# Cross-attention scores in four row groups of 32 instead of two of 64, with the opening and the seam of a one-core transformer kernel reordered

## The reference, cut to what matters

```python
x = x + _L0_xattn_ref(_layernorm(x, axis=-1), ctx_1024, itok_BxS_0_255, ...)   # 4 layers, 16 heads of 8
x = x + _L0_attn_ref(_layernorm(x, axis=-1), ternary_factor_u, ternary_factor_v)
...
allowed = (j[None, None, :] <= seg_ids[:, :, None]) & (j[None, None, :] > seg_ids[:, :, None] - LOOKBACK)
cross_bias = jnp.where(allowed, 0.0, NEG)[:, None]
for l in range(N_LAYERS):
    h = rmsnorm(x, n1[l]); ...                       # self-attention with rotation, x = x + o
    qc = split_heads(rmsnorm(x, n2[l]) @ Wq_c[l].T, H)
    kc, vc = jnp.split(memory @ Wkv_c[l].T, 2, axis=-1)   # split in heads too
    x = x + merge_heads(sdpa(qc, kc, vc, cross_bias)) @ Wo_c[l].T
    h3 = rmsnorm(x, n3[l]); x = x + jax.nn.silu(h3 @ Wg[l].T) * (h3 @ Wu[l].T) @ Wd[l].T
```

## Time and profile before

| | before |
|---|---|
| device time, median of 3 runs (lowest to highest) | 500.36 us (498.7 to 501.63) |
| profiled execution: device time, span | 499.64 us, 497.5 us |
| PE matmul busy, share of the span | 465.2 us, 94% |
| PE weight load | 401.7 us, 81% |
| DVE | 358.0 us, 72% |
| ACT | 268.5 us, 54% |
| POOL | 227.9 us, 46% |

### The profile page before, as it was taken

The page is one execution under the profiler, slowest core; times in us unless marked ns, Lnnn a source line. Parts: engine busy times, 40 slices in busy tenths (PEclk is TensorE's granted clock), DMA queues, the critical chain, the costliest instruction groups (busy, mean ns, idle before and its releaser), DMA issues. The chain is left out here.

```text
span 497.5 us, 14297 instructions
## 1 busy us (share of the span) xinstructions
PE 465.2 (94%) x5430; PEld 401.7 (81%) x5430; DVE 358.0 (72%) x1025; ACT 268.5 (54%) x718; POOL 227.9 (46%) x342
## 2 busy tenths in 40 slices
PE   3899999999999999968999998899999998999997
PEld 3667887788778876967999887789999887689997
DVE  4395668566856786656887889999989987654643
ACT  4377757775777577614334475556466554442221
POOL 2871377137613851243799322767889322300000
PEclk9999999999999999979999999999999999999999
DMA  8601020101029000040210432031020000000000
GB/s 252 276 3 32 10 84 2 40 22 65 3 64 381 2 3 1 2 130 17 70 49 24 157 111 67 2 133 60 10 69 3 2 1 1 1 2 1 12 1 12
DMA packets 9953, 27.08 MB, mean 54 GB/s; under 512 B 1346, under 2 KB 4759, under 8 KB 9623
## 3 DMA queue, kind: packets, MB, share of 16 engines
q1 hardware_dynamic: 9878, 26.09, 15.5%
HBM read 25.82 MB, written 0.26 MB: 52 GB/s over the span
## 5 line engine op out<-in xcount | busy, mean ns | idle before, releaser
L913 POOL TENSOR_TENSOR rstd<-ss,par 128x1 f32<-128x1 f32 x52 | 28.5, 549 | 100.8 <-ACT sq L737 100.8
L759 ACT ACTIVATE pr<-sd 128x512 f32<-128x512 f32 x56 | 34.5, 626 | 5.4 <-DVE sd L816 4.9
L1243 POOL TENSOR_TENSOR xh<-xh,rsx 128x512 f32<-128x512 f32 (+1 forms) x32 | 29.8, 931 | 2.5
L1241 POOL TENSOR_TENSOR xh<-cx,mvx 128x512 f32<-128x512 f32 (+1 forms) x32 | 29.4, 918 | 2.7 <-DMA cx<-ctx_in 1.4
L741 ACT ACTIVATE h<-y,rstd 128x128 f32<-128x128 f32 x48 | 19.1, 399 | 9.5 <-POOL rstd L913 9.4
L1222 DVE BATCH_NORM_STATS2 stx<-cx 128x6 f32<-128x128 f32 x104 | 22.7, 276 | 0.5 <-DMA cx<-ctx_in 0.5
L1772 POOL TENSOR_TENSOR rstd<-mv,par 128x1 f32<-128x1 f32 x20 | 4.1, 207 | 39.8 <-DVE mv L1602 36.3
L737 ACT ACTIVATE sq<-y 128x129 f32<-128x129 f32 x52 | 15.9, 306 | 10.0 <-DVE y L847 8.6
L907 POOL TENSOR_TENSOR kblk<-qk,cf 128x512 f32<-128x512 f32 x20 | 20.8, 1040 | 0.9
L1232 POOL TENSOR_TENSOR rsx<-rsx,par 128x13 f32<-128x13 f32 x8 | 20.4, 2546 | 0.6
L1791 POOL TENSOR_SCALAR rk<-kss 128x8 f32<-128x8 f32 (+1 forms) x32 | 7.5, 235 | 24.0 <-DVE kss L1668 22.5
(11 more groups left out here) (570 smaller groups left out, 1507.2 us busy)
## 6 DMA issues: line engine op xcount, KB each, us to landing
cx<-ctx_in SPq DMA_DIRECT2D x13, 768.0 KB
we<-we_in SPq DMA_DIRECT2D x8, 514.0 KB, 7.1
wc<-wc_in SPq DMA_DIRECT2D x4, 768.5 KB, 5.8
wa<-wa_in SPq DMA_DIRECT2D x5, 387.0 KB, 3.0
wb<-wb_in SPq DMA_DIRECT2D x4, 256.5 KB, 3.8
uvT<-uvT_in SPq DMA_DIRECT2D x1, 1024.0 KB, 7.1
uv<-uv_in SPq DMA_DIRECT2D x1, 1024.0 KB, 8.6
cx<-ctx_in SPq DMA_DIRECT2D x13, 32.5 KB
```

What stands on the lines that cost most here:

```text
L759: nc.scalar.activation(pr[:, t, at:at + 512], sd[:, t, at:at + 512], ACT.Exp).then_inc(s[piece], 1)
L913: nc.gpsimd.tensor_tensor(rstd[:, t:t + 1], ss[:, t:t + 1], par[:, 1:2], ALU.pow).then_inc(s[piece], 1)
L1241: step(pool, "pool_step", nc.gpsimd.tensor_tensor(part, cx[u % 2][:, tiles, :], mvx[:, b, tiles, 0].unsqueeze(2).to_broadcast(shape), ALU. ...
L1243: nc.gpsimd.tensor_tensor(part, part, rsx[:, b, tiles].unsqueeze(2).to_broadcast(shape), ALU.mult).then_inc(xm["c_normed"], 1)
```

## The change

1. `cmask` and `cscores` go by four row groups of 32 rows (4 heads) in four banks, 128 columns each, in place of two of 64 rows and 256 columns. `kcblk` is half as wide, `cmax` and `cshift` read four banks, and PSUM is two tensors of four banks.
2. Opening: x is loaded first; the flag comes from a row of ids of its own (2 KB), the ids of all partitions are loaded late; `mem4` moves from ACT to DVE, behind the layer norm; the zeroing moves from ACT to POOL. The four `memory` pieces of layer 0 and what follows from them get places of their own (`FIRST`), inside layer 0.
3. Seam: on PE the general form now stands ahead of the fast branch (`falls="end"`). ACT leaves the fast branch after its last `tanh` and DVE after `z_norm` of tile 1; what is left of the seam (`rest`) is issued behind the branch.
4. New places in both tables. The `memory` pieces of layers 1 to 3 move behind the query projection, to just ahead of `cmask` or `gate`.
5. Semaphore names of the general form share those of the fast branch, and 17 increments go from DVE's opening to the general form.

```diff
-PERIOD, SKEW = 95.43, (0.0, 6.74, 13.36, 19.85)
+PERIOD, SKEW = 94.56, (0.0, 6.67, 13.36, 19.85)
...
+FIRST = {"memory": 13.27, "mem_k": 12.13, "mem_v": 15.39, "kc": 12.61}
...
-    2: {"project": ("shifta", "shiftb"), "cmask": ("cshift",), "gate": ("hidden",)},
+    2: {"project": ("shifta", "shiftb"), "gate": ("hidden",)},
+    4: {"cmask": ("cshift",)},
...
-    return l * PERIOD + PLACE[p] + SKEW[t]
+    return l * PERIOD + (PLACE[p] if l else FIRST.get(p, PLACE[p])) + SKEW[t]
...
-        self.first = {e: 1 + max(n for n, z in enumerate(q) if z[1] == 0) for e, q in self.queue.items()}
+        self.first = {e: 1 + max(n for n, z in enumerate(q) if z[1] == 0 and not (e == "ACT" and z[2] == LAYERS) and
+                                 not (e == "DVE" and z[2] == LAYERS and z[3:] != (1, "z_norm"))) for e, q in self.queue.items()}
+        self.rest = {z[2:] for e, q in self.queue.items() for z in q[self.first[e]:] if z[1] == 0}
...
-        sc = [ctx.enter_context(nc.psum_tensor(f"sc{i}", [P, 1024], F32)) for i in range(2)]
-        pt = ctx.enter_context(nc.psum_tensor("pt", [P, 1024], F32))
-        sm = ctx.enter_context(nc.psum_tensor("sm", [P, 1024], F32))
+        fours = [ctx.enter_context(nc.psum_tensor(f"four{i}", [P, 2048], F32)) for i in range(2)]
+        sc = [fours[0][:, 0:1024], fours[0][:, 1024:2048]]
+        pt, sm = fours[1][:, 0:1024], fours[1][:, 1024:2048]
...
         def sp_opening(sp):
-            sp.dma_start(segr[:], seg_in.to_broadcast([P, B * L])).then_inc(s["seg_loaded"], 16)
             sp.dma_start(x[:], x_in.rearrange("(t p) d -> p t d", p=P)).then_inc(s["x_loaded"], 16)
+            sp.dma_start(segi[:], seg_in).then_inc(s["row_loaded"], 16)
+            sp.dma_start(cf[:], cf_in).then_inc(s["cf_loaded"], 16)
+            load_a(sp, 0)
             sp.dma_start(memT[:], memT_in).then_inc(s["mem_loaded"], 16)
             load_b(sp, 0)
-            sp.dma_start(cf[:], cf_in).then_inc(s["cf_loaded"], 16)
-            load_a(sp, 0)
             sp.dma_start(trig[:], trig_in).then_inc(s["trig_loaded"], 16)
             sp.dma_start(cb[:], cb_in).then_inc(s["trig_loaded"], 16)
+            sp.dma_start(segr[:], seg_in.to_broadcast([P, B * L])).then_inc(s["seg_loaded"], 16)
...
         def pool_opening(pool):
+            for blocks in (vblk, vcblk):
+                nc.gpsimd.memset(blocks[:], 0.0).then_inc(s["zeroed"], 1)
...
-            act.wait_ge(s["mem_loaded"], 16)
-            nc.scalar.copy(mem4[:], memT[:].unsqueeze(2).to_broadcast([P, B, 4, KF])).then_inc(s["zeroed"], 1)
-            for blocks in (vblk[:].rearrange("p t b j a e -> p (t b j a e)"), vcblk[:].rearrange("p b g i e -> p (b g i e)")):
-                nc.scalar.activation(blocks, par[:, 2:3].to_broadcast([P, B * 4 * 4 * 9]), ACT.Copy, scale=0.0).then_inc(s["zeroed"], 1)
...
-            dve.wait_ge(s["seg_loaded"], 16)
-            nc.vector.tensor_copy(segf[:], segr[:]).then_inc(s["seg_steps"], 1)
+            dve.wait_ge(s["zeroed"], 2)
+            for a in range(2):
+                nc.vector.memset(vblk[64 * a:64 * a + 64, :, :, :, a, 8:9], 1.0).then_inc(s["zeroed"], 1)
+            for a in range(4):
+                nc.vector.memset(vcblk[32 * a:32 * a + 32, :, :, a, 8:9], 1.0).then_inc(s["zeroed"], 1)
+            dve.wait_ge(s["row_loaded"], 16)
+            nc.vector.tensor_copy(pts[0:1, 0, 0:B * L], segi[:]).then_inc(s["seg_steps"], 1)
             dve.wait_ge(s["x_loaded"], 16)
...
+            dve.wait_ge(s["mem_loaded"], 16)
+            nc.vector.tensor_copy(mem4[:], memT[:].unsqueeze(2).to_broadcast([P, B, 4, KF])).then_inc(s["mem_spread"], 1)
+            dve.wait_ge(s["seg_loaded"], 16)
+            nc.vector.tensor_copy(segf[:], segr[:]).then_inc(s["cmask_set"], 1)
...
-                for p in range(2):
-                    rows = slice(L * p, L * p + L)
-                    nc.tensor.matmul(bank[:, 512 * p:512 * p + 256], cmask[rows, P * t:P * t + P], it32[rows, :], start=True, stop=True)
+                for p in range(4):
+                    rows = slice(KF * p, KF * p + KF)
+                    nc.tensor.matmul(bank[:, 512 * p:512 * p + P], cmask[rows, P * t:P * t + P], it32[rows, :], start=True, stop=True)
...
-                    for p in range(2):
-                        rows = slice(64 * p, 64 * p + 64)
-                        last = nc.tensor.matmul(bank[L * b:L * b + L, 512 * p:512 * p + 256], qT[rows, t, L * b:L * b + L],
+                    for p in range(4):
+                        rows = slice(KF * p, KF * p + KF)
+                        last = nc.tensor.matmul(bank[L * b:L * b + L, 512 * p:512 * p + P], qT[rows, t, L * b:L * b + L],
                                                 kcblk[rows, 2 * t + b, :, :], start=False, stop=True, skip_group_check=True)
...
-        def either(eng, fast, whole):
+        def either(eng, fast, whole, falls="start"):
...
-            with eng.If(few == 1):
-                fast()
+            with eng.If(few == (1 if falls == "start" else 0)):
+                (fast if falls == "start" else whole)()
             with eng.Else():
-                whole()
+                (whole if falls == "start" else fast)()
...
-                either(pe, lambda: opening(pe, x_pe_piece, pe_piece, "PE"), whole)
+                either(pe, lambda: opening(pe, x_pe_piece, pe_piece, "PE"), whole, falls="end")
```

More of the change, by code:

```diff
@@ new lines @@
+    "PE": {"memory": -47.35, "turn1": -4.73, "project": 0.00, "values": 2.11, "causal": 11.71, "scores": 13.88,
+           "turna": 21.45, "turnb": 23.00, "weigha": 23.32, "weighb": 26.86, "turn_o": 29.26, "out": 31.67,
+           "turn2": 37.19, "qc": 39.18, "cmask": 41.54, "cscores": 41.61, "cturn": 51.03, "cweigh": 52.61,
+           "cturn_o": 56.05, "cout": 58.70, "turn3": 65.72, "gate": 67.21, "up": 71.13, "down": 80.29},
+    "ACT": {"square1": -10.18, "norm1": -6.78, "mem_k": -41.75, "hT1": -3.24, "q_groups": 11.96, "expa": 19.12,
+            "expb": 21.79, "turneda": 23.14, "turnedb": 24.18, "oT": 30.28, "square2": 32.70, "norm2": 35.24,
+            "hT2": 37.60, "qcT": 40.50, "cexp": 47.98, "cturned": 52.37, "coT": 55.16, "square3": 60.48,
+            "norm3": 61.34, "hT3": 66.18, "tanh": 69.35},
@@ L75 @@
+    "DVE": {"mem_v": -37.82, "rope": 2.26, "vblk": 7.71, "maxa": 17.73, "maxb": 17.93, "shifta": 18.38,
+            "shiftb": 19.12, "recip": 28.46, "o": 29.58, "y1": 31.93, "cmax": 43.40, "cshift": 48.07, "crecip": 55.27,
+            "co": 55.93, "y2": 59.63, "gated": 72.85, "hidden": 76.84, "y3": 79.93},
+    "POOL": {"pow1": -28.06, "rope_sum": -12.13, "rope_bias": -9.86, "k_groups": -8.09, "base": 5.09, "kc": 14.77,
+             "pow2": 11.92, "pow3": 43.90},
 }
 PLACE = {p: a for pieces in AT.values() for p, a in pieces.items()}
+FIRST = {"memory": 13.27, "mem_k": 12.13, "mem_v": 15.39, "kc": 12.61}
@@ L122 @@
 LAYER = {e: list(pieces) for e, pieces in AT.items()}
-FINAL = {"PE": {}, "ACT": {"square_f": 0.18}, "DVE": {"norm_f": 4.73, "x_f": 6.55, "z_moments": 10.88, "z_norm": 17.41},
-         "POOL": {"pow_f": -7.85, "z_power": 0.96}}
+FINAL = {"PE": {}, "ACT": {"square_f": 0.83}, "DVE": {"norm_f": 5.32, "x_f": 9.97, "z_moments": 11.56, "z_norm": 18.17},
+         "POOL": {"pow_f": 14.74, "z_power": 27.05}}
 for e in AT:
@@ L150 @@
+YEACH = 20.703
 YAT = {
[L151 to L160 removed]
@@ L942, in queue @@
             for _, l, t, p in od.queue[engine]:
-                if within(p, l):
+                if within(p, l) and (l, t, p) not in JOINT.rest:
                     piece_of(eng, od, p, l, t)
@@ L1812, in x_queue @@
             fresh = False
-            for _, _, i, g, p in JOINT.queue[engine][JOINT.first[engine]:]:
+            for _, kind, i, g, p in JOINT.queue[engine][JOINT.first[engine]:]:
+                if kind == 0:
+                    layer_of(eng, FAST, p, i, g)
+                    continue
                 if p not in EARLY and not fresh:
@@ L1879, in whole @@
                 def whole():
+                    for name in sorted(set(gsem) - {"ctx_loaded"}):
+                        dve.sem_inc(gsem[name], 1)
                     dve.wait_ge(s["iota_loaded"], 32)
```

128 lines of the change are left out of this document (63 added, 65 removed).

## The result

| | before | after |
|---|---|---|
| device time, median (lowest to highest) | 501.0 us (498.7 to 502.9) | 511.51 us (508.35 to 2416.88) |
| profiled execution: device time, span | 499.64, 497.5 us | 508.35, 506.3 us |
| PE matmul busy | 465.2 us, 94% | 460.8 us, 91% |

The account below looks back on a forecast made before the run. PE's issued work bounds the layers, chains of waits the opening and the seam. Opening 1.4, scores 2.9 and seam 2.0 sum to 6.3 us: 493.3 against the profiled 499.64, 494.0 against the median; range 490 to 499.5.

Parts of the forecast that it names:

- opening: Before the layers: 6.0 us from a shorter chain, less 0.9 branch delay and 3.7 for `memory`: 1.4 won, -0.7 to 2.6.
- layers: Layers: four row groups for the scores shorten PE's work, 2.9 us won, between 9.4 lost and 4.3 won.
- seam: Seam: PE without its branch starts `across` earlier and at a better clock; 2.0 us won, between 0 and 3.7.
- price of a far branch: Opening: PE reaching its fast branch behind the general form costs 2.9 us; `turn1` 0.9 late, delay bounded by 0 and 3.
- The scores: Layers: `cscores` from 0.59 to 0.37 and 0.05 off `cmask`, 0.27 us saved per tile, 4.3 us of PE.
- the 0.48 of slack: Layers: gap between `cshift` of tile 0 ending and the next `cmask` starting stays 0.48 us in either order.
- the two thirds: Layers: share of the split's 4.3 us of PE taken to reach the end, 2.9 us.
- My upper bound: Seam: at most 3.7 us, from `across` starting 2.5 earlier plus 1.2 that the low clock costs the first `across`.
- The rest: Later blocks: pieces swap with neighbours only; 0 us, within 1.
- the second: Rival: PE's branch costs 2.9 in the opening, ACT's and DVE's branches take the seam's gain; 497.5 to 499.5, chance 0.20.
- my slower case: Rival: 32-row score records run at 74 ns each, 0.59 us lost per tile, 9.4 in all; 506 us, chance 0.08.

Follow-up runs that it names:

- run 9: The run 7 kernel with every load but x, ids, cf and wa held until the first `turn1` is done: 501.72 us, ratio 1.0037.
- run 5: Kernel of before with only `memory` of layers 1 to 3 moved to just ahead of `cmask` or `gate`, `mem_k` and `kc` along: 505.66 us, ratio 1.0098.
- run 3: Changed kernel with the scores in two row groups and two banks as before, new places kept: 508.65 us, ratio 1.0175.
- run 11: The run 10 kernel with `cmask` holding four banks until `cshift`, every product unchanged: 516.59 us, ratio 1.0363.
- run 7: Kernel of before with only the change's opening and seam, including general form first on PE; old places and score groups otherwise: 499.24 us, ratio 0.9966.
- run 10: The run 7 kernel with only wb, wc and the branch's own loads held until the first `turn1` is done: 494.54 us, ratio 0.9899.
- run 6: Kernel of before with only the change's opening, fast branch first on PE, no `rest`: 498.75 us, ratio 0.9947.
- run 1: Changed kernel with the fast branch first again on PE, the general form behind it: 508.84 us, ratio 1.0179.
- run 4: Changed kernel with the later blocks' places of before (`YWAY`, `YEACH`, `YAT`, `JOIN`): 504.35 us, ratio 1.0094.

## Why the prediction was wrong

The forecast for the profiled execution was 493.3 us, the measured time is 508.35, 15.1 more. In us won, by the lags above:

| | forecast | measured |
|---|---|---|
| opening | 1.4 | -2.2 |
| layers | 2.9 | -8.0 |
| seam | 2.0 | 5.1 |
| later blocks | 0 | -3.7 |

**The opening's mechanism was right, its price was not.** "I take that as the price of a far branch", 2.9 us from the seam. Measured against run 9, where the queues are empty, that is nearly right: flag to `turn1` is 10.78 - 6.31 = 4.5, and I had 4.0. In the changed kernel it is 8.4. I had named the busy transfers and then bounded the delay at 3 us, without working out how long the queue was. The loads issued ahead of the fetch, with the DMA engines at 1.00 and 364 GB/s from 8 to 12 us, were the thing to add up. The Trainium skill (Runtime: NRT & Kernel Launch, Instruction fetch mechanics) says that a taken branch out of the window forces a DMA fetch; the packets in the table of run 9 agree, and show that this fetch moves later when the kernel's own transfers are queued ahead of it.

**The scores: the size was right, where it would show was not.** 0.23 us a tile against 0.27; records of 32 rows took 26 ns, far from 74. The step that failed is "between lie `memory`, `qc` and `weighb` in either order, so the 0.48 of slack stays", and with it the two thirds that I took of the split's 4.3. I counted the slack at one wait, `cmask` on `cshift`. The same three pieces in the other order serve another wait, `qc` on `hT`: I even wrote that `memory` no longer covers `qc`, and gave it no price. The wait is some 0.35 us each time, and the moved `memory` pieces as a whole cost 2.1 us a layer in run 5, of which the waits are 0.9 and the rest is products that take longer in the new order. With all the new places it is 2.2 a layer (run 3), 6.6 of the 8 us. The trace of before had a sign of it: `memory` of tile 0, which I priced at 0.85 by the start of `qc`, takes 0.67 one tile later (43.21 to 43.88).

**Four banks.** I wrote that `gate` would depend on `cshift` of tile 3, and nothing more. Run 11 puts two more banks held at 20 us with the old order, some 6 us a layer. On the new order they cost some 1.2 us a layer (run 3), against 0.9 that the split saves. The new places are thus a trade: they cost 2.2 us a layer and take away most of what four banks would. With four banks there was no placing in these runs that kept the 48.7 us of before.

**Seam: undersized.** Forecast +2.0 of at most 3.7, measured 5.1. ACT's branch cost the chain nothing and DVE's lay under `across`. The branch alone does not fix the size: with the old places the same seam won 3.4 in run 7 and 5.1 in run 10, and the two differ in which products ran slow (`M` took 3.52 us in run 7 and 2.10 in run 10, both `across` 3.80 and 5.43). My upper bound counted only up to `across`; inside the first `M` PE had one more "issue" gap before, which is gone too:

```profile
226.03 1.87 PE L1277 MATMUL sc<-sd 64*64 64x64 f32 x113 [0.19 <-ACT sd L1456]
229.80 0.46 PE L1277 MATMUL sc<-sd 64*64 64x64 f32 x15 [1.89 <-issue]
```

Run 6, with the fast branch first, has 1.6 there, and run 1 has its second gap earlier, at the `z_turn` of tile 1. Each of these ends 2.6 to 2.9 us after a packet of the instruction queue (226.9 before, 224.7 in run 6, 223.4 in run 1), so they fit a second fetch behind the branch. No run tried that by itself.

**The rest, "0, within 1"**, was 3.7 by run 4. I had read that neighbours swap; the swap put the last relus ahead of 8 more updates at the one place with nothing behind them, the end.

Of the rivals, the second came nearest: the branch's stall moved into the opening; its other half, that ACT's and DVE's branches take the seam's gain, did not occur. None had a slower end by uncovered waits; my slower case, 74 ns a record, did not occur. Run 10 is close to what the forecast describes without its scores, 494.39 us in the profile where 1.4 + 2.0 would make 496.2, but it got there by luck: nothing won in the opening and 5.1 in the seam.

## What to carry to other kernels

When a piece moves behind another, list every wait that it covered before, not only the one it is moved for, and price each at what the waiting engine would stand there. An instruction fetch is a transfer: sum the bytes queued ahead of it, and look for its packet in the DMA view before putting an "issue" gap down to anything. Before using more PSUM banks for fewer columns, double the hold without changing a product, as in run 11: that one run gives the price of the banks, in the order of pieces that it is run with.
